# Shared expert of a four-layer block: ranks and places of group 0, GpSimd's power and VectorE's apply in another order

## The reference

```
router_logits = x @ gate_w.T                       # 16 experts
routing = softmax(router_logits)
topw, sel = top_k(routing, 2)
topw = topw / sum(topw)
hmid = silu(einsum('th,eih->tei', x, w1)) * einsum('th,eih->tei', x, w3)
moe_out = einsum('tei,ehi->th', hmid * combine, w2)
shared = silu(x @ ws_gate.T) * (x @ ws_up.T) @ ws_down.T
shared = sigmoid(x @ shared_gate_w.T) * shared
return moe_out + shared
```

## Time and profile before

| | us |
|---|---|
| median of 3 runs | 1770.66 (1765.32 to 1772.06) |
| the profiled execution | 1777.14 |
| its span, first to last instruction | 1775.4 |
| busy over the span: PE, DVE | 1534.9, 1332.9 |
| busy over the span: ACT, POOL | 1093.9, 1092.8 |

### The profile page before, as it was taken

One profiled execution on the slowest core, in us unless ns is written; L12 is line 12 of the kernel. 1 busy time (PEld: TensorE's weight loads), 2 busy tenths in 40 slices (PEclk: granted clock), 3 DMA queues, 4 the chain that ended last, 5 costly groups with the idle time before them and its releaser, 6 DMA issues.

```text
span 1775.4 us, 43982 instructions
## 1 busy us (share of the span) xinstructions
PE 1534.9 (86%) x14968; PEld 1236.2 (70%) x14968; DVE 1332.9 (75%) x2901; ACT 1093.9 (62%) x3516; POOL 1092.8 (62%) x1111
## 2 busy tenths in 40 slices
PE   7999999999999999989966755898895179999966
PEld 6888888888888888866645642565563079998855
DVE  6899998999998999866624434698886258887776
ACT  6888888888888888843325433655551056665610
POOL 5666666766667666646625554647777736665542
PEclk9999999999999999989989986999996589999988
DMA  8400000000000000022254425112213955554356
GB/s 242 125 11 20 20 20 20 20 20 20 20 17 14 20 20 20 8 102 83 82 169 150 151 73 173 49 38 94 83 68 117 320 164 165 159 161 146 120 200 274
DMA packets 103082, 167.67 MB, mean 94 GB/s; under 512 B 20223, under 2 KB 75980, under 8 KB 102480
## 3 DMA queue, kind: packets, MB, share of 16 engines
q1 hardware_dynamic: 77136, 105.37, 19.4%
q0 software_dynamic: 22272, 56.15, 8.6%
q10 hardware_dynamic: 3456, 3.34, 0.6%
HBM read 95.31 MB, written 75.76 MB: 96 GB/s over the span
## 4 chain that ended last, share of the span: by engine, by line
PE 66%; DVE 11%; issue 9%; POOL 5%; another core or an unknown queue 3%; ACT 2%; DMA 1%; SPq 1%; ACTq 1%; DVEq 0%; POOLq 0%
PE layers_banks L321 14%; PE layers_banks L292 13%; PE layers_banks L307 9%; PE layers_banks L888 8%; PE layers_banks L899 4%; PE layers_banks L1267 3%; PE layers_banks L275 3%; PE layers_banks L281 3%; PE layers_banks L876 2%; POOL l_rows_in L1177 2%; DVE weights L1860 2%; POOL l_by_token L1008 2%; PE layers_banks L1280 1%; PE layers_banks L2151 1%
## 5 line engine op out<-in xcount | busy, mean ns | idle before, releaser
L466 POOL TENSOR_TENSOR w_down<-w_down,layers_arena 128x1024 f32<-128x1024 f32 x256 | 483.5, 1894 | 233.7 <-DVE layers_arena L420 232.6
L387 ACT ACTIVATE w_down<-layers_banks,layers_arena 128x256 f32<-128x256 f32 x1024 | 468.6, 496 | 2.3 <-DVE layers_arena L414 2.3
L1008 POOL DMA_INDIRECT l_by_token<-layers_arena x240 | 245.4, 1022 | 195.2 <-issue 97.8
L425 DVE COPY w_down<-layers_banks 128x1024 f32<-128x1024 f32 x256 | 312.3, 1220 | 40.7 <-PE layers_banks L307 36.7
L414 DVE TENSOR_REDUCE layers_arena<-layers_banks 128x4 f32<-128x1024 f32 x256 | 309.6, 1210 | 27.0 <-PE layers_banks L292 26.8
L292 PE MATMUL layers_banks<-layers_arena 64*128 64x256 f32 x2048 | 279.7, 385 | 1.6 <-ACT w_down L387 0.9
L321 PE MATMUL layers_banks<-w_down,layers_arena 128*64 128x256 f32 x2048 | 250.8, 387 | 1.5 <-DVE w_down L425 1.3
L387 ACT ACTIVATION_READ_ACCUMULATOR w_down<-layers_banks,layers_arena 128x1 f32 x1024 | 236.4, 231 | 0.0
L888 PE MATMUL layers_banks<-layers_arena 128*128 128x128 f32 x1600 | 203.5, 279 | 34.6 <-ACT layers_arena L931 28.8
L1177 POOL DMA_INDIRECT l_rows_in<-layers_arena,l_routing_group_slots x192 | 189.4, 986 | 57.7 <-issue 44.9
L307 PEld LDWEIGHTS layers_banks<-ident,w_down 64*128 64x128 f32 x4096 | 169.1, 138 | 77.4 <-issue 71.6
(11 more groups left out here) (227 smaller groups left out, 2551.6 us busy)
## 6 DMA issues: line engine op xcount, KB each, us to landing
layers_arena<-l_rows_in SPq DMA_DIRECT2D x240, 136.0 KB
weights<-l_by_token SPq DMA_DIRECT2D x32, 512.0 KB, 9.8
layers_arena<-in_ctx SPq DMA_DIRECT2D x64, 128.0 KB, 2.8
layers_arena<-l_by_token SPq DMA_DIRECT2D x32, 256.0 KB, 2.9
weights<-in_w_gu SPq DMA_DIRECT2D x16, 512.0 KB
l_rows_in<-zeros SPq DMA_DIRECT2D x1, 4352.0 KB
x_sb<-in_x SPq DMA_DIRECT2D x32, 128.0 KB, 2.6
w_down<-in_w_down SPq DMA_DIRECT2D x1, 4096.0 KB
```

Source lines behind the costliest of these rows:

```text
L387: last = nc.scalar.activation(prob[:, n % 4, c, :], ps_s[:, n % 2, c, :], ACT.Exp, bias=negmax[:, n % 2, c:c + 1], accum_out=sums[:, n % 2 ...
L425: nc.vector.tensor_copy(prob_t[:, n // 2 % 2, n % 2, :, :, :].rearrange("p k c (d s) -> p d (k c) s", d=2), ps_t[:, :, :, :].rearrange("p ...
L466: nc.gpsimd.tensor_tensor(prob[:, n % 4, :, :], prob[:, n % 4, :, :], rsum[:, n % 2, :].unsqueeze(2).to_broadcast([P, 4, A_N]), ALU.mult). ...
L1008: pool.indirect_dma_start(m.by_token, bass.IndirectOffsetOnAxis(ap=place, axis=0), outs[:, r % OUTS, b, :], None, bounds_check=T * m.K - 1 ...
```

## The change

Three orders are changed; no work is added or taken away. (1) TensorE makes the ranks of group 0 ahead of the first gate and up half instead of behind it, and VectorE makes the places of group 0 ahead of the statistics of group 2 instead of behind them. (2) GpSimd's power of group g + 2 moves from ahead of the scatter of group g to between its two rounds, behind `mark_sent`. (3) VectorE's apply of group g + 2 moves from ahead of the two hidden products to behind them, and so directly ahead of `choose`.

```diff
@@ TensorE, step @@
-            gate_up_half(it, q, 0)
             if g == 0:
                 rt.make_ranks(pe, it, q, done)
+            gate_up_half(it, q, 0)
@@ VectorE, step @@
+            if g == 0:
+                rt.place_rows(dve, it, q, done)
             if exists(it, q + 2):
                 norm_statistics(nc, dve, x_sb, it, q + 2, stats, mv, vare, norm_steps, passed)
-            rt.place_rows(dve, it, q, done)
+            if g > 0:
+                rt.place_rows(dve, it, q, done)
             if g == NG - 1:
                 tables_sizes(dve)
-            if exists(it, q + 2):
-                apply(it, q + 2)
             for f in range(2):
...
                 nc.vector.tensor_tensor(hidden[:, q % 2, f, :], silu[:, f, :], ps_gu[:, f, 1, :], ALU.mult)\
                     .then_inc(h_ready[f], 1)
+            if exists(it, q + 2):
+                apply(it, q + 2)
             done(dve, sg_ready, it, q)
@@ GpSimd @@
         for g in range(NG):
-            if g + 2 < NG:
-                deviation(g + 2)
             rt.scatter(pool, g // 2, g % 2, xn[:, g % DEPTH, :, :], 0, 2 * g, done)
             if g > 0:
                 rt.mark_sent(pool, (g - 1) // 2, (g - 1) % 2)
+            if g + 2 < NG:
+                deviation(g + 2)
             rt.scatter(pool, g // 2, g % 2, xn[:, g % DEPTH, :, :], 1, 2 * g + 1, done)
```

## The result

The changed kernel takes 1793.14 us (median of 4 runs, 1791.9 to 1801.97) where the kernel before takes 1771.36 (4 runs, 1765.32 to 1773.84). The ratio of the runs, as it is on record, is 1.0153, with a 95% interval of 1.0126 to 1.0181: slower by 22 to 32 us. (The quotient of the two medians is 1.0123, or 21.8 us.) The forecast was 15.7 us slower, 1786.4, with a range up to 1797. The sign and the place are right, the size is not.

The account below looks back on a forecast made before the run. TensorE, plus VectorE's last residual add once per group, was taken to bound the shared-expert stage; 2.3 us (group 0) + 13.4 (waits in steps 1 to 5) = 15.7, on 1770.66 giving 1786.4 us, range 1780 to 1797.

Parts of the forecast that it names:

- The wait: Shared-expert steps 1 to 5: late power makes TensorE's transposes wait 2.67 us more each step, 13.4 us in all.
- the hand-over from apply to transposes: Last link from slots to transposes: 0.26 us from the end of VectorE's apply, within a path of 8.36 us.
- the spacing of the issues: GpSimd's scatter round: issues taken as 1.26 us apart by their starts, not 0.96, so the fourth comes after 4.41.
- the row behind the transposes: On TensorE, down products, ranks and the next gate-up follow the transposes, so the 2.67 us wait returns in each step.
- The clock: TensorE, steps 1 to 5: forecast no loss; rival had waits lowering the clock, 5 x 1.7 = 8.6 us, 1795; one in five.
- rows 8: Profile rows of TensorE idle times: clock stayed 1.00 behind 2.44 us, 0.57 behind 3.15; the new wait was about 2.6.
- the sign of being wrong: Profile after the change: a granted clock under 1.00 behind TensorE's waits would show the forecast wrong.
- Hides: VectorE's choose, 2.54 us behind the late apply, ends 0.5 us before the residual add can start, so costs nothing.
- Group 0: Step 0: slots 3 us earlier, but power waits for the scatter round; transposes 2.3 us later, TensorE's own delay hidden.
- The end: Steps 6 and 7 of the shared-expert stage: same as before, forecast 0 us.

Follow-up runs that it names:

- run 3: Changed kernel with the transposes of group g+1 repeated twice on TensorE to fill its wait; stage 147.1 us, ratio 1.0104 to the kernel before.
- run 4: Changed kernel with the apply back ahead of the hidden products and the power between second and third issue of round 0; stage 131.4 us, ratio 1.0016.
- run 5: Changed kernel with TensorE's down products ahead of the transposes of group g+2; stage 135.3 us, ratio 1.0045 to the kernel before.
- run 1: Changed kernel with the power of group g+2 back ahead of round 0 of the scatter; stage 147.0 us, ratio 1.0089 to the kernel before.
- run 8: As run 2, with the logits of group g+1 moved between the two gate-up halves; stage 148.9 us, ratio 1.0081 to the kernel before.
- run 2: Changed kernel with the apply back ahead of the two hidden products; stage 154.1 us, ratio 1.0116 to the kernel before.
- Run 6: Kernel before with only group 0's new order (ranks ahead of gate-up, places ahead of statistics); stage 132.0 us, ratio 1.0011.

## Why the prediction was half right

**The wait.** Right, link by link: the power behind the fourth issue (5.62), power to apply 1.09, the wait repeated in steps 1 to 5, steps 6 and 7 without it. The one link too long was the hand-over from apply to transposes, 0.26 by the first transposes of the stage; in step 1 it was 821.05 - 819.61 - 1.38 = 0.06. With the clock held at 1.00, in run 3, a step is 16.7 us, where the forecast had 16.9. Runs 4 and 5 confirm the two halves of the argument: the spacing of the issues, and the row behind the transposes.

**The clock.** The step that failed is the choice between rows 8: "My 2.6 stands nearer to the 2.44". By it the sum put the clock at nothing, where it measured 11.4 us, and the sign of being wrong that the prediction itself named, a granted clock under 1.00 behind the waits, came. Idle times were compared by their length, and not by what TensorE did before them. The wait was even shorter, 2.31, and the clock fell in each of five steps; in run 1 it fell behind 1.01. The 2.44 of rows 8 lies in another stage, behind other products. Run 8 speaks for the work ahead of the wait, with four steps of five; what decides in each case (step 1 of run 8, step 0 of the changed kernel) stays open. The Trainium skill's page "TensorE: Matmul & The Clock Gate" (HAM oscillation) tells of a loop that waits between its groups of matmuls and starts each group cold; the trace agrees, with transposes of 1.97 for 1.07 in five steps of five. Run 8 does so in one step of five only. One chance in five was far too little. Its price was mis-sized too: 1.7 was read from one fall; here the loss was 1.5 to 1.6 in two steps and 2.7 to 2.9 in three, where the clock stayed low longer into the down products, together 11.4 and not 8.6.

**The apply behind the products.** "Hides" was wrong as a statement on that part, though with the power late it made little difference in steps 1 to 5 (run 2). I followed what is behind the apply on VectorE (choose) and not who else waits for it: the transposes, which were ready at 8.65 after gate-up, while the second hidden product ends at 8.5 and the apply of 1.38 comes behind it. Run 1 shows it: a wait of 1.0, and the clock with it. In the whole change the late power covers this in steps 1 to 5.

**Group 0.** The size was near (3.2 for 2.3) by luck; the reason was another. I had the power as the last to come and TensorE's own delay hidden under it. Step 0 after the change (TensorE, then VectorE):

```profile
792.83 8.78 PE L1267 MATMUL layers_banks<-layers_arena,weights 128*128 128x512 f32 x16
...
804.32 1.09 PE L1257 MATMUL layers_banks<-ident,layers_arena 128*128 128x128 f32 x8 [1.01 <-DVE layers_arena L1466]
...
802.28 0.69 DVE L1381 TENSOR_TENSOR layers_arena<-layers_arena,layers_banks 128x512 f32<-128x512 f32 x1 [2.74 <-ACT layers_arena L1343]
...
802.88 1.38 DVE L1466 TENSOR_SCALAR layers_arena<-x_sb,layers_arena 128x256 f32<-128x256 f32 x4
```

Gate-up takes 8.78 us: ahead of its ranks TensorE waits 0.84 us for the mask while its clock is low, and the clock is back over 3 us later, counted from the first transposes, than before. Then silu, the second hidden product and the apply follow on one another, and the apply (802.88) waits for nothing: the power had come at 801.7. Run 6 has the same late rise without the other two parts, and with it 2.3 of the 3.2 us. The other 0.9 goes with the apply behind the products: step 0 takes 26.8 to 26.9 us where the apply stands there (after, run 1), and 26.0 to 26.1 where it stands ahead and TensorE's order is the same (runs 2, 4 and 6).

**The end.** The 2.2 us gained there were not foreseen. TensorE's rest ahead of group 7's gate-up is shorter (3.07 for 3.96), and behind it the first half took 3.70 at full clock in place of 5.40. The shorter rest doesn't explain the clock: the same half took 5.40 behind a rest of 3.04 in run 1 and behind one of 1.87 in run 8. Why the clock stayed up there is open, and it is not shown that the 2.2 us come from the change.

## What to carry to other kernels

When a row moves on one engine, list everyone who waits for its result, not just what is queued behind it: here the apply had a second reader, TensorE's transposes, with 2.3 us of slack, and two of the three moves each spent more than that. A new wait on TensorE is to be priced with the clock behind it, by rows in which the same work stands ahead of the wait, and not by the length of the wait alone; even such rows leave a spread, as step 0 did here. And where a late input can't be helped, work that doesn't need it goes ahead of the wait: one swap on TensorE returned 20 of 24.7 us in the changed kernel, and made the old one's stage 5.5 us shorter.

## What the runs showed of the hardware

- The granted clock fell behind a wait of 1.01 us that followed the logits, in steps 1 to 5 (run 1), but not behind one of 1.01 in step 0 (after). It stayed at 1.00 in four of five behind a wait of 2.2 that followed a gate-up half (run 8), and in five of five where transposes filled all but 0.52 of the wait (run 3).
- Behind equal waits of 2.31 the fallen clock cost unequal amounts, in turn: 2.9 us in step 1 and 1.6 in step 2 (after; in run 2 such steps took 18.2 and 19.3 us in turn).
- Indirect DMA issues follow one another on GpSimd 1.26 us from start to start, though a row is 0.96: taking two of them out of the way moved the apply by 2.5 us (7.14 after gate-up in run 4, 9.66 in run 2). The power starts 0.98 behind the start of the last issue (817.54 to 818.52), so the 0.30 stands ahead of a further issue, not behind each.
